# Mixture-of-experts stage of a two-layer transformer kernel: from all experts on all tokens to 19 blocks of tokens sorted by expert

## The reference

```python
logits = x @ W_router                       # x: 2048 x 256, after a layernorm; 4 experts
expert_idx = jnp.argmax(logits, axis=-1)
h = jnp.einsum('th,ehi->tei', x, W1) + b1   # all four experts, inner width 1024
h = jax.nn.gelu(h, approximate=False)
onehot = jax.nn.one_hot(expert_idx, E, dtype=x.dtype)
intermediate = jnp.einsum('te,tei->ti', onehot, h)
y = intermediate @ Wo + bo + x              # Wo is shared by the experts
y = _layer_norm(y, ln_gamma, ln_beta)
# and outside: x = x + tanh(g_ffn[1]) * y
```

## Time and profile before

| | us |
|---|---|
| Median of 3 runs (929.94 to 940.11) | 939.09 |
| The profiled execution's own time | 938.04 |
| Its span, first to last instruction | 936.2 |
| PE busy | 837.2 (89%) |
| DVE busy | 577.3 (62%) |
| ACT busy | 438.8 (47%) |
| POOL busy | 249.8 (27%) |

### The profile page before, as it was taken

The page is one execution under the profiler, slowest core; times in us unless marked ns, Lnnn a source line. Parts: engine busy times, 40 slices in busy tenths (PEclk is TensorE's granted clock), DMA queues, the critical chain, the costliest instruction groups (busy, mean ns, idle before and its releaser), DMA issues. The chain is left out here.

```text
span 936.2 us, 11844 instructions
## 1 busy us (share of the span) xinstructions
PE 837.2 (89%) x4356; PEld 498.8 (53%) x4356; DVE 577.3 (62%) x932; ACT 438.8 (47%) x821; POOL 249.8 (27%) x277
## 2 busy tenths in 40 slices
PE   6875999999989889976999999955999999999985
PEld 3432443433336678742443333313778778778764
DVE  4664899889426936576889999648704135136026
ACT  2322788888755476512778877863210210210110
POOL 2230554554533275500000000124211120120220
PEclk9996899999999999986899999995998998998998
DMA  7695222222032200352245222010000000000000
GB/s 269 183 211 153 69 70 70 70 69 70 2 110 80 82 1 0 88 163 69 66 126 179 88 70 70 19 46 2 1 0 1 1 23 1 1 23 1 0 23 23
DMA packets 40538, 60.67 MB, mean 65 GB/s; under 512 B 7256, under 2 KB 17240, under 8 KB 40480
## 3 DMA queue, kind: packets, MB, share of 16 engines
q1 hardware_dynamic: 37216, 55.84, 20.1%
q0 software_dynamic: 864, 0.92, 1.3%
q10 hardware_dynamic: 2400, 3.15, 1.0%
HBM read 40.02 MB, written 18.87 MB: 63 GB/s over the span
## 5 line engine op out<-in xcount | busy, mean ns | idle before, releaser
L1118 DVE TENSOR_REDUCE row_max<-ps_wide 128x2 f32<-128x1024 f32 x256 | 301.0, 1219 | 34.4 <-PE ps_wide L479 28.0
L829 ACT ACTIVATE probs<-ps_a 128x512 f32<-128x512 f32 x342 | 192.9, 605 | 44.3 <-PE ps_a L535 40.4
L479 PE MATMUL ps_wide<-stack_k,stack_q 48*128 48x512 f32 x512 | 155.4, 468 | 14.8 <-DVE row_max L1118 11.1
L535 PE MATMUL ps_a<-stack_q,stack_k 62*128 62x512 f32 (+1 forms) x342 | 140.2, 459 | 10.9 <-ACT probs L829 10.9
L549 PE MATMUL ps_out<-probs,vals 128*17 128x512 f32 x1024 | 135.9, 604 | 3.0 <-POOL probs L978 0.5
L932 ACT ACTIVATE hid_full<-ps_a 128x512 f32<-128x512 f32 x32 | 19.1, 598 | 221.6 <-PE ps_a L748 156.1
L535 PEld LDWEIGHTS ps_a<-stack_q,stack_k 62*128 62x128 f32 (+1 forms) x342 | 61.2, 191 | 100.1 <-ACT probs L829 70.1
L829 ACT ACTIVATE probs<-ps_misc 128x512 f32<-128x512 f32 x170 | 102.9, 606 | 20.7 <-PE ps_misc L535 16.5
L978 POOL TENSOR_TENSOR probs<-probs,fixes_sb 128x512 f32<-128x512 f32 x64 | 81.9, 1279 | 85.7 <-ACT probs L829 85.7
L1037 POOL TENSOR_TENSOR hid_lo<-hid_full,hid_hi 128x512 fp32r<-128x512 f32 x32 | 42.5, 1331 | 198.3 <-ACT hid_hi L933 198.3
L479 PEld LDWEIGHTS ps_wide<-stack_k,stack_q 48*128 48x128 f32 x512 | 66.3, 192 | 49.8 <-DVE row_max L1118 20.7
(11 more groups left out here) (166 smaller groups left out, 1244.3 us busy)
## 6 DMA issues: line engine op xcount, KB each, us to landing
planes_k<-planes SPq DMA_DIRECT2D x32, 256.0 KB, 3.9
planes_q<-planes SPq DMA_DIRECT2D x32, 256.0 KB, 3.7
stack_q<-planes_q SPq DMA_DIRECT2D x64, 128.0 KB, 2.8
stack_k<-planes_k SPq DMA_DIRECT2D x64, 128.0 KB, 2.8
stack_q<-planes_q SPq DMA_DIRECT2D x64, 64.0 KB, 2.7
stack_k<-planes_k SPq DMA_DIRECT2D x64, 64.0 KB, 2.6
w_e_raw<-in_L_W SPq DMA_DIRECT2D x4, 1024.0 KB, 5.2
w_raw<-in_L_W SPq DMA_DIRECT2D x2, 1024.0 KB, 6.2
```

Source lines behind the costliest of these rows:

```text
L479: mm(raw_slot(("pair", g, p))[:, i * S:(i + 1) * S], stack_q[at, slot(g, c) + q * P:slot(g, c) + (q + 1) * P], stack_k[at, slot(g, c):slot ...
L535: mm(score_slot(("tile", n))[:], stack_k[at, slot(g, c) + k * P:slot(g, c) + (k + 1) * P], stack_q[at, slot(g, c):slot(g, c) + S], start=T ...
L829: do(probs[n % PROBS][:, j, :], score_slot(("tile", n * HG + j))[:], ACT.Exp, scale=0.25).then_inc(exp_done, 1)
L1118: v.tensor_reduce(row_max[:, g % 2, :, p], raw_slot(("pair", g, p))[:].rearrange("p (i k) -> p i k", i=2), AX, ALU.max).then_inc(sem(f"max ...
```

## The change

The last stage no longer runs all experts on all tokens. It sorts the tokens by expert on the chip and runs 19 blocks of 128 sorted rows, each with one expert's weights (16 full blocks and up to 3 more for ends that are not full; 19 are always run). In words:

- Routing now comes first for all four batches: PE makes the logits, DVE the one-hot rows, and PE counts with small matmuls against a triangle and a matrix of ones (`count`). DVE gets the slot of each token (`place`) and small tables (`tables`): the expert of each block and where its list starts.
- POOL writes the token numbers to HBM with 16 indirect DMAs of 128 numbers (`place_ids`), reads 19 lists of 128 back with one, and PE turns them.
- PE reads 19 offsets into registers (`value_load`), and addresses W1 with them in every up matmul.
- SP stores the normalised rows and x to HBM (`keep_rows`). POOL gathers 128 rows of both for each block by an indirect DMA, and scatters 128 finished rows to the output by another. Rows without a token have an index out of bounds and are not moved.
- In a block the rows are the stationary operand of the up product (12 matmuls of 512 hidden columns and 2 with biases), so hidden rows come out token by token and are turned by 8 PE transposes before the down product. The low part of the hidden rows is now DVE's, not POOL's.
- Splitting the weights moves: POOL splits experts 0 and 2 inside the second attention's end, ahead of the roots of `roots(3, b)`; ACT and DVE split experts 1 and 3. `normal(3, 0)` and `normal(3, 1)` move into DVE's part of the attention.

The diff, cut to what the prediction speaks of:

```diff
@@ sync
+                             (table[:], a["table"]), (sums[:], a["sums"])):
                 sp.dma_start(dst, src).then_inc(sem("w_moe"), 16)
+            def keep_rows(b):
+                to = rows_dram[b * S:(b + 1) * S, :].rearrange("(t p) d -> p t d", p=P)
+                sp.wait_ge(sem("normed"), 3 * T + QT * (b + 1))
+                for i, rows in enumerate((xn, x)):
+                    sp.dma_start(to[:, :, i * D:(i + 1) * D], rows[:, b * QT:(b + 1) * QT, :]).then_inc(sem("rows_kept"), 16)
@@ tensor
+            pe.wait_ge(sem("normalised1"), G)
+            turn_n3(0)
+            route_logits(0)
+            for b in range(1, B):
+                turn_n3(b)
+                route_logits(b)
+                count(b - 1)
+            count(B - 1)
+            pe.wait_ge(sem("counts_kept"), B)
+            mm(ps[1][:, 0:E], sums[:, 1, :], running[:, B - 1, 0, :], start=True, stop=True).then_inc(sem("totals"), 1)
+            pe.wait_ge(sem("ids_back"), 16)
+            tr(ps[0][:, 0:BLOCKS], ids_rows[0:BLOCKS, :], ident[0:BLOCKS, 0:BLOCKS]).then_inc(sem("ids_turned"), 1)
+            pe.wait_ge(sem("table_step"), 11)
+            at = [nc.tensor.value_load(offset[0:1, i:i + 1], min_val=0, max_val=(E - 1) * C * FF) for i in range(BLOCKS)]
...
+            def up(n):
+                wait(pe, sem("hid1_ready"), 2 * (n - 1))
+                for half in range(2):
+                    bank = pw[n % 2][:, half * S:(half + 1) * S]
+                    for i, (r, w) in enumerate(PRODUCTS):
...
+                        for c in range(C):
+                            mm(bank, sortedT[r][:, n % 2, c, :], w1_flat[w][:, bass.ds(at[n] + (c * FF + half * S), S)],
+                               start=(i == 0 and c == 0), stop=False)
+                    mm(bank, select[0:HOT, n, :], b1_parts[0:HOT, half * S:(half + 1) * S], start=False, stop=True
+                       ).then_inc(sem("up1_done"), 1)
...
+            for n in range(BLOCKS):
+                up(n)
+                if n + 1 < BLOCKS:
+                    turn_rows(n + 1)
+                if n > 0:
+                    down(n - 1)
+                turn_hidden(n)
+            down(BLOCKS - 1)
@@ gpsimd
                 if l == 1:
+                    pool.wait_ge(sem("w_moe"), 16 * (E + 7))
+                    pool.wait_ge(sem("scores_done1"), (G - 2) * QT * HG)
+                    for i, e in enumerate(EARLY):
+                        for q in range(4):
+                            cols = slice(q * S, (q + 1) * S)
+                            v.tensor_copy(w1_hi[:, e, cols], w1_raw1[:, e, cols]).then_inc(sem("w1_high"), 1)
+                            pool.wait_ge(sem("w1_high"), 4 * i + q + 1)
+                            v.tensor_tensor(w1_lo[:, e, cols], w1_raw1[:, e, cols], w1_hi[:, e, cols].bitcast(F32), ALU.subtract
+                                            ).then_inc(sem("w1_low"), 1)
                     for b in range(B - 1):
                         roots(3, b)
...
+            for n in range(ROW_RING - 1):
+                gather(n)
+            for n in range(BLOCKS):
+                root4(n)
+                if n > 0:
+                    scatter(n - 1)
+                m = n + ROW_RING - 2
+                if n > 0 and m < BLOCKS:
+                    wait(pool, sem(f"stored_{m % ROW_RING}"), 16 * (m // ROW_RING))
+                    gather(m)
+            scatter(BLOCKS - 1)
@@ vector
+                    if l == 1 and g == G + 1:
+                        normal(3, 0, x)
+                        normal(3, 1, x)
...
+            v.memset(sorted_rows[:], 0.0).then_inc(sem("b1_cleared"), 1)
...
+            for n in range(BLOCKS + 2):
+                if n + 1 < BLOCKS:
+                    rows_low(n + 1)
+                if 0 < n <= BLOCKS:
+                    residual(n - 1)
+                if n < BLOCKS:
+                    hidden_low(n)
+                if n > 1:
+                    finish(n - 2)
+                if 0 < n <= BLOCKS:
+                    spread(n - 1)
```

More of the change, by code:

```diff
@@ L13 @@
 F16 = mybir.dt.float16
+U32 = mybir.dt.uint32
+I32 = mybir.dt.int32
 P = 128
@@ new lines, in turn_hidden, with down @@
+            def turn_hidden(n):
+                for half in range(2):
+                    pe.wait_ge(sem("hid1_ready"), 2 * n + half + 1)
+                    wait(pe, sem("hid1_low"), 2 * n - 1 + half)
+                    for f in range(FC // 2):
+                        at_f = (half * FC // 2 + f) * P
+                        last = tr(ps[half][:, f * P:(f + 1) * P], hid1[:, n % 2, at_f:at_f + P], ident[:])
+                    last.then_inc(sem("hid1_turned"), 1)
+            def down(n):
+                wait(pe, sem("down1_read"), n)
@@ L756, in _ @@
[L756 to L764 removed]
+                        last = mm(po[:, 0:D], hid1T[r][:, n % 2, f, :], w_mo_parts[w][:, f, :],
+                                  start=(f == 0 and i == 0), stop=(f == FC - 1 and i == 2))
@@ L926, in _ @@
-            for b in range(B):
-                wait(act, sem("down1_done"), QT * b)
-                for f in range(FC):
-                    u = b * FC + f
-                    act.wait_ge(sem("up1_done"), u + 1)
-                    wait(act, sem("hid1_low"), u - 1)
-                    do(hid1_full[:, u % 2, :], ps[u % 2][:], ACT.Gelu)
-                    do(hid1[0][:, f, :], ps[u % 2][:], ACT.Gelu).then_inc(sem("hid1_high"), 1)
-                    if b < B - 1 and f == 2:
-                        rows1(b + 1)
+            rows1(2)
@@ new lines, in _ @@
+            route(0)
+            normal(3, B - 1, x)
+            place(0)
+            for b in range(1, B):
+                route(b)
+                place(b)
+            for i, e in enumerate(LATE):
+                weights_low(i, e)
+            tables()
+            dve.wait_ge(sem("b1_high"), 1)
+            v.tensor_tensor(b1_parts[32:HOT, :], b1_raw[32:HOT, :], b1_parts[32:HOT, :], ALU.subtract).then_inc(sem("b1_split"), 1)
+            dve.wait_ge(sem("ids_turned"), 1)
+            v.tensor_copy(ids[:], ps[0][:, 0:BLOCKS]).then_inc(sem("ids_ready"), 1)
@@ new lines, in finish @@
+            def finish(n):
+                t = n % T
+                w, r, h, y1 = (z[:, t:t + 1] for z in (var_eps, root, newton, rstd))
+                st, k = sem("newton_step"), 4 * (4 * B + n)
+                dve.wait_ge(sem("root_ready"), k // 4 + 1)
+                v.tensor_tensor(h, r, r, ALU.mult).then_inc(st, 1)
+                dve.wait_ge(st, k + 1)
+                v.tensor_tensor(h, h, w, ALU.mult).then_inc(st, 1)
+                dve.wait_ge(st, k + 2)
+                v.tensor_scalar(h, h, -0.5, 1.5, ALU.mult, ALU.add).then_inc(st, 1)
+                dve.wait_ge(st, k + 3)
+                v.tensor_tensor(y1, h, r, ALU.mult).then_inc(st, 1)
+                dve.wait_ge(st, k + 4)
+                rows, back = y[:, n % 2, :], sorted_rows[:, n % ROW_RING, D:2 * D]
+                v.tensor_scalar(rows, rows, meanvar[:, t, 0:1], y1, ALU.subtract, ALU.mult).then_inc(sem("scaled"), 1)
```

498 lines of the change are left out of this document (278 added, 220 removed).

## The result

The changed kernel takes **1019.3 us** (median of 5 runs, 1011.4 to 1024.8), the kernel before, beside it, 935.2 (5 runs, 929.9 to 940.1). The ratio is 1.087, 95% interval 1.082 to 1.092: slower by 8 to 9%, far outside the forecast range of 845 to 905. The profiled execution, the quickest of the five (1011.4), has a span of 1009.5 us.

What follows compares the result with a forecast made beforehand. It took PE's matmuls in the last stage as the bound. First up product at 690, 19 x 8.0 = 152, 3 for clock and 2.5 for ends give 847.5; tail 7.8 and 2.9, span 858, plus 1.8: 860 us, range 845 to 905.

Steps and rivals of the forecast that it cites:

- One block: Last stage: up, down, ten transposes and joints take PE 8.0 us a block; PE sets the pace, 19 x 8.0 = 152.
- B: POOL's DMAs cost 2.9 us each; the start is 30 us later, 890 us, and the loop holds; chance 0.14.
- C: PE's clock stays at 1.2 GHz in the loop: a block of 14.3 us, 980 us; chance 0.06.
- The slow side: Whole kernel slower than before by over 1%; chance 0.09.
- A's lock between DVE and POOL: In the loop DVE and POOL exclude each other, DVE sets the pace: block 8.9 us, 877 us; chance 0.17.
- The start: Before the loop: routing, placings, lists and register loads put the first up product at 690, 39 us later than before.
- The placings: After routing: 1.0 us per issue on POOL; the last four end their issue at 675 and land at 677.
- the row I took: PE's register loads at the start, priced by SP's issue of 0.43 us: 19 x 0.43 = 8.2 us, 4 us showing.
- The tail: After the last down product: 7.8 us on DVE and 2.9 for a scatter.

Runs made afterwards that it cites:

- six-buffer kernel: The changed kernel with ROW_RING, the ring of gathered rows, at 6 buffers in place of 5: 882.9 us (4 runs), ratio 0.941 to the kernel before.
- the reordered one: The changed kernel, five buffers, with POOL issuing the gather of block n+3 ahead of the root of block n: 900.8 us (one run).
- the run that kept it up: The changed kernel, five buffers, with 48 unused PE products ahead of each wait for gathered rows from block 5 on: 990.9 us (one run).

## Why the prediction was wrong

**The step that failed** is in "One block": "so the chain fits. PE sets the pace." It checked the chain of one block (turned hidden rows, ACT, DVE, down), and summed each engine's work: PE 8.0, DVE 6.1, POOL 2.6. The sums were near: 7.9, 5.5 and 2.6 in the six-buffer kernel. What it never drew is the chain that leaves the block and comes back: down, residual and spread on DVE, root, scatter, gather, landing, turning of rows, down. One turn takes 16.7 us, and five buffers allow one turn per block. Had the gather been followed to its user, the prediction's own numbers gave nearly this: 2.9 down, 6.1 on DVE, 2.6 on POOL, 3.9 landing and 0.3 turning make 15.8, for each block. The six-buffer kernel and the reordered one show that this loop is the cause, 136 and 118 us. In the profile the stage from the first up product (702.4) to the last down product's end (993.3) takes 290.9 us instead of 157.5. These 133.4 are nearly all of the miss in the span (1009.5 instead of 858); 12.4 lie in the start and 5.5 in the tail.

**The rivals.** None was it. B named `sorted_rows` as the wait that would show, but by the price of a DMA's issue, and that was 1.0 us as forecast. C had a true core at the wrong place: the clock does fall, yet since PE waits; it is 2 of the 9 us per block by the run that kept it up, and it came back to 1.00 with the sixth buffer. The slow side got 0.09 of chance; with a loop across blocks unpriced, that was far too little.

**What held.** The block: in the changed kernel the up products of blocks 1 to 3, whose rows had landed early, start 7.9 us apart (711.08, 719.00, 726.90), and so do the blocks from there on in the six-buffer kernel; forecast 8.0. The stage in that kernel, from the first up product (710.56) to the last down product's end (863.6), takes 153.0 against 157.5. Register-addressed weights cost little: the six products of a half take 1.56 us there (804.05 to 805.61) where 6 x 0.235 makes 1.41, and no run shows whether the registers make the difference. A's lock between DVE and POOL does not set the block's pace; where it does appear is the start, 3.06 for an issue of 0.96. The page "SBUF — State Buffer" of the Trainium skill, section "Who interferes with whom", has a DVE instruction with two inputs in SBUF contend with GpSimd instructions that read SBUF, but lists `tensor_tensor` as one that did not stall DMAs and infers that it leaves descriptor generation alone. The trace agrees with the first and not with the second, and the measurement decides: two-input subtractions (TENSOR_TENSOR) are what held the issues of indirect DMAs here.

**The start**, forecast 690, measured 702.4 in a profile whose earlier stages happened to be quick:
- PE got going at 630.4, not 638: POOL's pairs took 1.9 each, not 2.1, and began at 607.3, not 613.
- A batch of routing took 8.2 us (644.83 to 653.03), not 7.4: four of them ended on PE at 665.9 instead of 667.6.
- The placings: the last issue ended at 676.0, forecast 675, since DVE's hold on POOL gave back what routing was early. They landed at 685, not 677. This is the term that was mis-sized most: one DMA's plain landing of 2 to 3 us was taken for 128 pieces of 4 bytes, which signal after 9 to 15.
- The lists back at 688.3 (3.3 after issue, forecast 2.9). Register loads 12.7 us for 19, 0.67 each, not 0.43. The Trainium skill's floor in "DMA: Bandwidth & Descriptors", section "Latency and other measured facts", would have made an estimate of 11.4; it was nearer than the row I took. The load itself is 0.30 here, and two further instructions and gaps make the rest. All of it showed, since it stood behind the wait; ahead of it, the first up product comes 7.4 instead of 14.1 us after the ids, and what is left is the first gather.

**The tail**, forecast 10.7 from the last down product to the end, is 16.2 in the six-buffer kernel (863.6 to 879.8): DVE 9.2 instead of 7.8, 0.8 to the scatter's issue at 873.56, and from there to the end 6.2 instead of 2.9.

By these terms the six-buffer kernel can be summed: 690 + 153 + 16.2 + 1.8 = 861 with the forecast start, 882 with the measured 710.6. So the forecast of 860 was the price of a kernel with one more buffer and a better start, and not of this one.

## What to carry to other kernels

When work is spread over queues in a software pipeline, sum each engine, and then draw every chain that leaves a block and returns: its length divided by the number of blocks by which one turn moves on is a bound like any engine's. Here that number is the buffers less four: the gather runs three blocks ahead of the root with five buffers, and its rows are turned two blocks ahead of the down product, so with five buffers one turn leads from block n's root only to block n+1's. A prefetch behind a result in an in-order queue is no prefetch; one buffer more, or the order of two lines, was worth 118 to 136 us here. And put long loads of registers ahead of the wait, not behind it.

## What the hardware showed that was not expected

- An indirect DMA took POOL 0.95 to 1.06 us to issue (1.13 for the first placing), with 0.30 to the next, whether it moved 4 bytes or 2 KB for each index; beside DVE's subtraction of 128x2048 the same instruction took up to 3.06, and beside one of 4x1024 up to 1.81.
- 128 placings of 4 bytes each signal 9 to 15 us after their issue ended; gathers of 128 rows of 2 KB landed 2.7 to 6.0 us after theirs began (median 3.4). The DMA engines' share was 0.01 in the 22 us from 666 on.
- A register load from memory on PE costs 0.67 us one after another (0.30 the load, 0.15 and 0.02 the two that follow).
- After 6.4 us of waiting, 24 down products took 5.3 us at a clock of 0.54; with 6.0 us of unused products in the wait, 3.1 us at 1.00.
